# Weights joined early in a second attention, and its blocks chained behind the picks of a routed layer

## The reference

```python
x = x + _L0_ffn_ref(_layernorm(x), ...)
# second attention, block by block (128 tokens attend 128 context rows)
Q = einsum('btx,dx->btd', layernorm(x), Wq) + bq
K = einsum('bpx,dx->bpd', features, Wk) + bk
scores = einsum('btd,bpd->btp', Q, K) / sqrt(512)
attended = einsum('btp,bpd->btd', softmax(scores), features)
x = x + attended
x = x + _L1_ffn_ref(layernorm(x), ...)
```

## Time and profile before

| | |
|---|---|
| median of 3 runs | 1229.75 us (1226.36 to 1233.53) |
| profiled execution | 1234.57 us |
| its span | 1232.8 us |
| TensorE busy | 957.1 us (78%) |
| VectorE busy | 750.1 us (61%) |
| ScalarE busy | 470.8 us (38%) |
| POOL busy | 422.6 us (34%) |
| mean granted TensorE clock | 0.867 |

### The profile page before, as it was taken

The page is one execution under the profiler, slowest core; times in us unless marked ns, Lnnn a source line. Parts: engine busy times, 40 slices in busy tenths (PEclk is TensorE's granted clock), DMA queues, the critical chain, the costliest instruction groups (busy, mean ns, idle before and its releaser), DMA issues. The chain is left out here.

```text
span 1232.8 us, 15264 instructions
## 1 busy us (share of the span) xinstructions
PE 957.1 (78%) x5115; PEld 660.6 (54%) x5115; DVE 750.1 (61%) x1190; ACT 470.8 (38%) x671; POOL 422.6 (34%) x360
## 2 busy tenths in 40 slices
PE   5888758779999999316881338989987758868997
PEld 2655525556666666105761217854445435546886
DVE  5677373967777777484137973357755467734444
ACT  2444323236666666112221214334431145524230
POOL 5344031146666666233121264010002041216631
PEclk9899677889999999757895658989998879988999
DMA  7000111337777665722110013000000120013000
GB/s 284 2 1 2 52 49 43 120 107 257 249 262 281 236 238 191 301 98 85 35 60 0 1 51 105 32 19 1 1 1 1 69 111 1 1 35 103 35 18 35
DMA packets 31982, 110.09 MB, mean 89 GB/s; under 512 B 4321, under 2 KB 4641, under 8 KB 28577
## 3 DMA queue, kind: packets, MB, share of 16 engines
q1 hardware_dynamic: 24384, 84.47, 19.0%
q0 software_dynamic: 7520, 24.65, 6.2%
HBM read 130.07 MB, written 16.78 MB: 119 GB/s over the span
## 5 line engine op out<-in xcount | busy, mean ns | idle before, releaser
L1035 POOL DMA_INDIRECT f_picks<-f_turn_xn,f_target x47 | 117.0, 2489 | 68.4 <-ACT f_turn_xn L975 68.1
L1337 PE MATMUL banks<-f_t_dn,f_z 128*128 128x512 f32 x188 | 88.5, 593 | 0.6 <-issue 0.6
L164 PE MATMUL banks<-ident,a_turn_xn 128*128 128x128 f32 x64 | 16.2, 413 | 76.4 <-DVE a_turn_xn L172 76.4
L106 POOL TENSOR_TENSOR a_ahead_var_eps<-mean_var,eps 128x1 f32<-128x1 f32 x32 | 6.3, 197 | 192.6 <-DVE mean_var L102 192.6
L1171 DVE TENSOR_TENSOR f_gu_lo<-f_t_gu,f_gu_hi 128x2048 fp32r<-128x2048 f32 x24 | 55.0, 2294 | 12.5 <-ACT f_gu_hi L961 11.6
L1029 POOL DMA_INDIRECT f_turn_xn<-f_xn_rows,f_token x47 | 47.5, 1011 | 40.6 <-DVE f_token L1165 17.9
L1171 DVE TENSOR_TENSOR f_xn_lo<-f_t_gu,f_xn_hi 128x2048 fp32r<-128x2048 f32 x23 | 52.7, 2292 | 12.2 <-ACT f_xn_hi L961 12.2
L164 PEld LDWEIGHTS banks<-ident,a_turn_xn 128*128 128x128 f32 x64 | 11.2, 209 | 81.9 <-DVE a_turn_xn L172 81.8
L2146 ACT ACTIVATE a_e<-banks 128x1024 f32<-128x1024 f32 x32 | 32.8, 1024 | 52.2 <-PE banks L2245 52.1
L961 ACT CAST f_gu_hi<-f_t_gu 128x2048 fp32r x24 | 45.7, 1906 | 9.1 <-DMA f_t_gu<-in_f_gu 6.4
L968 ACT ACTIVATE f_sil<-banks 128x256 f32<-128x256 f32 x47 | 18.1, 384 | 79.8 <-PE banks L244 79.8
(11 more groups left out here) (441 smaller groups left out, 2867.9 us busy)
## 6 DMA issues: line engine op xcount, KB each, us to landing
f_t_gu<-in_f_gu SPq DMA_DIRECT2D x47, 1024.0 KB
f_t_dn<-in_f_dn SPq DMA_DIRECT2D x47, 512.0 KB
f_t_gu<-f_picks SPq DMA_DIRECT2D x6, 1024.0 KB, 8.3
raw<-in_ctx_rows SPq DMA_DIRECT2D x4, 1024.0 KB, 5.0
f_xn_rows<-f_turn_xn SPq DMA_DIRECT2D x9, 256.0 KB, 2.3
x_res<-in_x SPq DMA_DIRECT2D x8, 256.0 KB, 6.0
a_ctx<-in_ctx SPq DMA_DIRECT2D x2, 1024.0 KB, 13.0
a_out_mask<-in_mask SPq DMA_DIRECT2D x1, 2048.0 KB, 15.8
```

What stands on the lines that cost most here:

```text
L164: mm = pe.transpose(self.core.psum[:, self.first_bank + b % 2, c * P:(c + 1) * P], self.xn[:, b % self.rows, c * P:(c + 1) * P], self.core ...
L1035: pool.indirect_dma_start(dram["f0_picks_flat"], bass.IndirectOffsetOnAxis(ap=target[:, t:t + 1], axis=0), t_y[:, t % F0_BUFS, :], None).t ...
L1337: mm = pe.matmul(ps[:, TY_BANK + t % 2, :], t_zt[:, t % 2, c, :], t_dn[:, t % F0_BUFS, c, :], start=c == 0, stop=c == F0_IC - 1)
```

## The change

The second attention is no longer a function of its own; its work stands in `l0_ffn`, in plain fp32.

- Wkᵀ and Wq in another layout are loaded into `raw` while the routed layer's jobs run. `join` makes their product (4 outputs of 4 chunks, 128x512 each), two outputs ahead of `down`, two behind `tokens`; `join_vec` makes what the biases give (36 products with one moving column). ScalarE copies them out.
- The turned context (two loads of 1 MB) is loaded behind tile 5's down weights, the context rows behind the last tiles. For each half of the context, `keys` makes four outputs and one row of 512 columns, 20 products of 128x512 in all: those of half 0 directly behind the last tile, those of half 1 five at a time in the steps of blocks 0 to 3.
- The picks are loaded three blocks at once. VectorE's loop over steps adds two picks of block s, normalizes block s-1, adds two more, makes the statistics of block s, adds the attended rows of block s-2 and makes the maxima of block s-1. TensorE's step turns the exponentials of block s-2 and the rows of block s-1, makes three key products, attends block s-2, makes the scores of block s-1 (five products of 128 columns) and two key products.
- The statistics behind the attention go to a second set of tiles (`late`).
- The next part's weights are prefetched behind the last tile's down weights.

```diff
+                sp.dma_start(a_bias[:, :, :], dram["a1_bias"]).then_inc(a_bias_loaded, 16)
+                sp.wait_ge(gu_lo_ready, 1)
+                sp.dma_start(core.raw[:, 0, :], dram["a1_wk"]).then_inc(a_w_loaded[0], 16)
+                sp.wait_ge(dn_lo_ready, 1)
+                sp.dma_start(core.raw[:, 1, :], dram["a1_wq"]).then_inc(a_w_loaded[1], 16)
...
+                    if t == 2 * F0_BUFS:
+                        sp.wait_ge(a_joined_done, NC)
+                        sp.wait_ge(a_vec_done, 1)
+                        for h in range(HALVES):
+                            sp.dma_start(a_ct[:, h, :, :].rearrange("p c n -> p (c n)"), dram["ctx_turned"][h])\
+                              .then_inc(a_ct_loaded[h], 16)
                 load_dn(F0_TILES - 1)
                 core.prefetch(sp, "f0")
+                sp.wait_ge(t_gu_done, F0_TILES)
+                sp.dma_start(chunked(a_rows[1]), dram["ctx_rows"][1]).then_inc(a_rows_loaded[1], 16)
+                sp.wait_ge(t_y_done, F0_TILES)
+                sp.dma_start(chunked(a_rows[0]), dram["ctx_rows"][0]).then_inc(a_rows_loaded[0], 16)
...
+                def take_joined(c):
+                    act.wait_ge(a_joined_done, c + 1)
+                    act.copy(a_joined[:, c, :], ps[:, c, :]).then_inc(a_joined_ready, 1)
+                def take_vec():
+                    act.wait_ge(a_vec_done, 1)
+                    act.mul(a_vec[:, 0:2 * NC], ps[:, VEC_BANK, 0:2 * NC], a_scale).then_inc(a_vec_ready, 1)
+                    act.mul(a_vec[0:1, 2 * NC:], ps[0:1, VEC_BANK, 2 * NC:2 * NC + 1], a_scale)\
+                       .then_inc(a_vec_ready, 1)
...
+                def take_keys(n):
+                    half, m = divmod(n, KEY_JOBS)
+                    act.wait_ge(a_keys_done, n + 1)
+                    bank = JOB_BANK + n % 2
+                    if m == NC:
+                        ins = act.activation(a_row[:, half * HT:(half + 1) * HT], ps[0:1, bank, :], ACT.Identity,
+                                             bias=a_vec[0:1, 2 * NC:], scale=1.0)
+                    else:
+                        if half == 1 and m == 0:
+                            for i in range(F0_BUFS):
+                                act.wait_ge(t_stored[i], 16 * len(range(i, F0_TILES, F0_BUFS)))
+                        ins = act.activation(a_keys(half, m), ps[:, bank, :], ACT.Identity,
+                                             bias=a_vec[:, NC + m:NC + m + 1], scale=a_scale)
+                    ins.then_inc(a_keys_ready, 1)
...
+                act.wait_ge(y_done, B)
+                take_joined(0)
+                take_joined(1)
                 act.wait_ge(owner_ready, 3)
                 tile_gu_hi(0)
+                take_joined(2)
+                take_joined(3)
+                take_vec()
                 tile_gu_hi(1)
                 tile_x(0)
                 for t in range(F0_TILES):
@@ -1004,6 +1121,19 @@
                     if t >= 1:
                         tile_y(t - 1)
                 tile_y(F0_TILES - 1)
+                for n in range(KEY_JOBS):
+                    take_keys(n)
+                for s in range(1, B + 2):
+                    if s >= 2:
+                        exponentials(s - 2)
+                        take_turned(s - 2)
+                    if s <= B:
+                        take_rows(s - 1)
+                    if s <= HB:
+                        take_keys(KEY_JOBS + s - 1)
+                    if s == HB:
+                        take_keys(KEY_JOBS + s)
...
-                for b in range(B):
-                    dve.wait_ge(picks_loaded[b], 16)
-                    for k in range(F0_TOPK):
-                        if k:
-                            dve.wait_ge(picks_added, F0_TOPK * b + k)
-                        dve.scalar_tensor_tensor(out=core.x[:, b, :], in0=picks[b % len(picks)][:, k, :],
-                                                 scalar=weight[:, b, k:k + 1], in1=core.x[:, b, :],
-                                                 op0=ALU.mult, op1=ALU.add).then_inc(picks_added, 1)
-                    dve.wait_ge(picks_added, F0_TOPK * (b + 1))
-                    ahead.dve(dve, b)
+                for s in range(B + 2):
+                    if s < B:
+                        dve.wait_ge(picks_loaded[s], 16)
+                        add_pick(s, 0)
+                        add_pick(s, 1)
+                    if 1 <= s <= B:
+                        rows(s - 1)
+                    if s < B:
+                        add_pick(s, 2)
+                        add_pick(s, 3)
+                        dve.wait_ge(picks_added, F0_TOPK * (s + 1))
+                        ahead.dve(dve, s)
+                    if s >= 2:
+                        add_attended(s - 2)
+                    if 1 <= s <= B:
+                        maxima(s - 1)
...
+                def join(c):
+                    pe.wait_ge(a_w_loaded[0], 16)
+                    pe.wait_ge(a_w_loaded[1], 16)
+                    pe.wait_ge(z_ready, F0_JOBS if c >= 2 else F0_JOBS - 1)
+                    for d in range(NC):
+                        mm = pe.matmul(ps[:, c, :], a_wk[:, d, c * P:(c + 1) * P], a_wq[:, d, :],
+                                       start=d == 0, stop=d == NC - 1)
+                    mm.then_inc(a_joined_done, 1)
...
+                    pe.wait_ge(a_bias_loaded, 16)
+                    pe.wait_ge(sigmoid_ready, 1)
+                    for i, w in enumerate((a_wk, a_wq)):
+                        for c in range(NC):
+                            for d in range(NC):
+                                pe.matmul(ps[:, VEC_BANK, i * NC + c:i * NC + c + 1], w[:, d, c * P:(c + 1) * P],
+                                          a_bias[:, 1 - i, d:d + 1], start=d == 0, stop=d == NC - 1)
+                    for d in range(NC):
+                        mm = pe.matmul(ps[0:1, VEC_BANK, 2 * NC:2 * NC + 1], a_bias[:, 1, d:d + 1],
+                                       a_bias[:, 0, d:d + 1], start=d == 0, stop=d == NC - 1)
+                    mm.then_inc(a_vec_done, 1)
...
+                    if m == NC:
+                        mm = pe.matmul(ps[0:1, bank, :], a_vec[:, c:c + 1], a_ct[:, half, c, :],
+                                       start=c == 0, stop=c == NC - 1)
+                    else:
+                        mm = pe.matmul(ps[:, bank, :], a_joined[:, c, m * P:(m + 1) * P], a_ct[:, half, c, :],
+                                       start=c == 0, stop=c == NC - 1)
+                    if c == NC - 1:
+                        mm.then_inc(a_keys_done, 1)
...
+                def scores(b):
+                    half, i = divmod(b, HB)
+                    pe.wait_ge(a_keys_ready, KEY_JOBS * (half + 1))
+                    pe.wait_ge(a_xt_ready, b + 1)
+                    if b:
+                        pe.wait_ge(a_exp_ready, b)
+                    at = slice(i * P, (i + 1) * P)
+                    for c in range(NC):
+                        pe.matmul(ps[:, S_BANK, 0:P], a_xt[:, b % 2, c, :], a_keys(half, c)[:, at],
+                                  start=c == 0, stop=False)
+                    pe.matmul(ps[:, S_BANK, 0:P], a_ones, a_row[:, b * P:(b + 1) * P], start=False, stop=True)\
+                      .then_inc(a_scores_done, 1)
+                def turn_e(b):
...
+                join(0)
+                join(1)
                 down()
                 tokens()
+                join(2)
+                join(3)
+                join_vec()
                 pe.wait_ge(y_added, B)
+                pe.wait_ge(a_joined_ready, 1)
                 tile_turn(0)
                 for t in range(F0_TILES):
                     tile_gu(t)
@@ -1360,251 +1632,32 @@
                     tile_turn_z(t)
                 tile_down(F0_TILES - 1)
+                for n in range(KEY_JOBS):
+                    for c in range(NC):
+                        keys(n, c)
+                for s in range(1, B + 2):
+                    if s >= 2:
+                        turn_e(s - 2)
+                    if s <= B:
+                        turn_rows(s - 1)
+                    if s <= HB:
+                        for i in range(KEY_JOBS * (s - 1), KEY_JOBS * (s - 1) + 3):
+                            keys(KEY_JOBS + i // NC, i % NC)
+                    if s >= 2:
+                        attend(s - 2)
+                    if s <= B:
+                        scores(s - 1)
+                    if s <= HB:
+                        for i in range(KEY_JOBS * (s - 1) + 3, KEY_JOBS * s):
+                            keys(KEY_JOBS + i // NC, i % NC)
+        core.next = 1 - core.next
...
-    out["a1_wk"], out["a1_wq"] = rows(a["L1_xattn_Wk"].T), rows(a["L1_xattn_Wq"].T)
+    out["a1_wk"], out["a1_wq"] = rows(a["L1_xattn_Wk"]), rows(a["L1_xattn_Wq"])
...
-            l1_attention: [dram["a1_wk"], ct[0]], l1_ffn: [dram["f1_w"], dram["f1_cols"]],
+            l1_ffn: [dram["f1_w"], dram["f1_cols"]],
```

365 lines of the change are left out of this document (139 added, 226 removed).

## The result

The changed kernel takes 1175.62 us (median of 4 runs, 1172.55 to 1182.78), the kernel before beside it 1231.64 us: ratio 0.957, 95% interval 0.950 to 0.963, so 56 us less, as forecast. The profiled execution took 1173.74 us against 1234.57.

What follows compares the result with a forecast made beforehand. The kernel was taken as a chain of stages, TensorE filling the routed tiles and idling around them. Gain 77.0 us, delay 17.0 and clock allowance 4 gave -56: from 1229.75 to 1174 us, range 1160 to 1196.

Steps and rivals of the forecast that it cites:

- The sum: Whole kernel: 77.0 us gained behind the tiles, 17.0 delay ahead of them, 4 for a falling clock: -56 us.
- Joins 0 and 1: Behind the last job, in the down product's gap: 8 products, 6.9 us, delaying the tokens by only 0.85 us.
- Joins 2 and 3: Behind the tokens, ahead of tile 0: 8 products, 6.9 us, until 254.7.
- The vectors: join_vec ahead of tile 0: 72 one-column rows, clock falling halfway, 12.1 us.
- Rival 3: Ahead of tile 0: joins and vectors run at 1.2 GHz, delay 27.2 us, total 1184; chance 0.15.
- The picks: Behind the last tile: context rows' load shares the queues, so picks come at 513.6 instead of 512.60, between 0 and 3 later.
- The blocks: Attention loop: first round 9 us, then 8.5 to block 3, 6.7 for later ones, last 4.4; 4 us allowed for clock.
- Rival 2: Whole kernel: the clock never falls, delay 13.4 us and no 4 us at the end, total 1166; chance 0.17.
- Rival 4: Block loop runs cold throughout, rounds of blocks 0 to 3 13.5 us instead of 8.5, total 1197; chance 0.13.
- Rival 5: Attention blocks don't overlap, each costing the sum over engines, total 1253, slower than before; chance 0.03.
- Rival 6: Work made early isn't early: keys of half 0 start only at the first block's turn, total 1202; chance 0.02.
- The rule against the row: join_vec: the skill read plainly keeps 2.4 GHz, an earlier trace row shows small products losing it; weight loads alone give 7.7 us.

Runs made afterwards that it cites:

- the two controls: The changed kernel run again unedited, in the first and the last set: 1172.29 and 1175.22 us, 0.9518 and 0.9544 of the kernel before.
- joins behind: The changed kernel with joins 0 and 1 moved out of the down product's gap to behind the tokens: 1192.60 us, 0.9693 of the kernel before.
- Rows late: The changed kernel with both context row loads issued behind the first three loads of picks instead of ahead: 1174.40 us, 0.9522 of the kernel before.
- unchained: The changed kernel with all picks of all blocks added before the attention's loop begins: 1198.08 us, 0.9693 of the kernel before.

## Why the prediction was right

- **The sum** was -77.0 + 17.0 + 4 = -56; the profile has -73.1 behind the tiles (155.9 to 82.8, clock included, forecast -73.0), +13.7 ahead of them and +0.5 in them: -58.9, and 2.3 us elsewhere. The medians of the first comparison say -56.0, with an interval of the ratio that reaches from 45 to 62 us, the ratios of the two controls (0.9518, 0.9544) -59 and -56. The way of the gain is as forecast; that the median meets the sum to the microsecond is luck: the delay ahead of the tiles was 3.3 us off, two errors of 3 us behind them cancelled, and the profiled executions differ by 60.8.
- **Joins 0 and 1** were priced at 0.85 us: VectorE's add stands at J + 8.45 against 7.61, and "joins behind" gave 0.83 of it back. **Joins 2 and 3**: 6.93 us, forecast 6.9.
- **The vectors** are a term that was mis-sized: 12.1 us forecast, 9.1 measured, within its bounds 8.5 to 15.3. The prices of a row with 128 columns of weights held: 0.112 at full and 0.213 at half clock measured, 0.118 and 0.213 taken. Two things were missed. The clock fell behind some 48 of the 72 rows and not behind 34 (1.3 us), and the last 8 rows, bias by bias with one column of weights, took 0.025 us each and not 0.213 (1.5 us). The lower full-clock price makes the rest of the 3.0. Rival 3, cold early work, is refuted: 13.7 of delay, not 27.2. Behind the vectors the queue took 5.7 us, forecast 5.95.
- **The tiles** were to be unchanged: 247.9 against 247.45. Not foreseen was that their cold start (before too: 0.77 for the first product in the earlier trace rows) can be avoided, worth 1.7 to 1.8 us by the sixth tile.
- **The picks** were mis-sized: 1 us for the context rows' load, bounds 0 to 3, measured 4.7 (14.1 against 9.45). "Rows late" shows the cause, and its size. I had the mechanism, and priced only the picks' landing, not the scatters ahead of the issue. The 20 keys took 17.4 us, forecast 17.2, and ended 3.4 us ahead of block 0's rows, not behind them: the path to block 0 ran through the picks and not, as forecast, through the keys. So one sign of being wrong, VectorE waiting for picks, was met at block 0 (16.17 us against 11.51 before), and at no later block.
- **The blocks**: rounds 9.49, 8.03, 8.31, 6.25, 6.7 and 4.38 against 9, 8.5, 8.5, 6.7 and 4.4. The clock fell in the last four as allowed for (0.76 from 573 to 587), but the maxima stayed under 6.8 apart: VectorE, busy 12.5 of those 14 us, hid the slower products. From the first maximum to the next layer 57.5 us, forecast 56.6 warm and 60.6 with the allowance: 3 us too long, which paid for the 3 us too short ahead of it. The two errors have nothing to do with one another.
- **Rival 2**, a clock that never falls, is out: it fell ahead of tile 0 and again in the last blocks. **Rival 4**, rounds of 13.5, is out in blocks 0 to 3 in all kernels. **Rival 5**, no overlap: even unchained the kernel is 3% faster than before. **Rival 6**: keys start within 0.2 us of the last tile.
- **The rule against the row.** The Trainium skill ("TensorE: Matmul & The Clock Gate", What's actually happening) has activity release the half rate, so that a join_vec without a gap stays fast. The trace disagrees with that reading: TensorE was busy without a gap from 245.4 to 261.4 and lost the clock between 257 and 258. It was at 0.50 for the rest, as the row at 598 to 604 in the earlier trace rows had warned. The weight load that the Trainium skill gives on the same page (LDWEIGHTS, 107 ns for 128 columns) is near at full clock (112 ns from row to row) and not at half (213 ns). The prediction's 7.7 us for 72 such rows also counted the 8 with one column of weights, which took 25 ns each.

Of the 73 us behind the tiles, 19 are the chaining by blocks and 18 the keys under the wait for picks, each undone by itself. The other 36 (no query projection, no splitting, no border between the layers) weren't tried one by one; their sum is all that is shown, and only if the 19 and the 18 add up, which no run with both edits shows.
